# Attention with turned weights against scores made a second time in turned form, on one core

## The reference

```
h = attention(x): 16 heads of 32; q, k, v = x Wq', x Wk', x Wv'
    scores = q k' / sqrt(32);  scores = -inf where mask (512 x 512, one for all batches)
    o = softmax(scores) v;  o = o Wo'
    h = o / rms(o) * rms_scale * (1 + sc[b]) + shift[b]     (sc, shift from the conditioning)
x = x + h
x = x + quaternion rotation of x with a spectral gate       (a fixed 512 x 512 map, 4 x 4 blocks)
```

## Time and profile before

| | us |
|---|---|
| median of the runs | 988.85 |
| span of the profiled execution | 986.2 |
| median less span | 2.7 |
| TensorE matmul busy | 912.2 (92%) |
| TensorE weight load busy | 648.2 (66%) |
| VectorE busy | 707.5 (72%) |
| ScalarE busy | 638.8 (65%) |
| GpSimd busy | 523.6 (53%) |

### The profile page before, as it was taken

The page is one execution under the profiler, slowest core; times in us unless marked ns, Lnnn a source line. Parts: engine busy times, 40 slices in busy tenths (PEclk is TensorE's granted clock), DMA queues, the critical chain, the costliest instruction groups (busy, mean ns, idle before and its releaser), DMA issues.

```text
span 986.2 us, 20466 instructions
## 1 busy us (share of the span) xinstructions
PE 912.2 (92%) x6278; PEld 648.2 (66%) x6278; DVE 707.5 (72%) x1581; ACT 638.8 (65%) x1523; POOL 523.6 (53%) x441
## 2 busy tenths in 40 slices
PE   7999999999968989999999998999999999999980
PEld 5788888888845557666666665666666666666650
DVE  4522132223168888989999898899999899898878
ACT  5222222223158888888888887788888888888820
POOL 0999930000001122677666776566677666776665
PEclk9999999999979999999999999999999999999995
DMA  8855465544878547756666745666665576455111
GB/s 282 303 188 193 170 223 189 183 171 181 186 249 185 118 98 181 164 117 151 150 140 139 194 108 129 152 155 145 142 161 125 133 187 156 109 120 139 33 54 43
DMA packets 82325, 153.98 MB, mean 156 GB/s; under 512 B 8472, under 2 KB 9112, under 8 KB 82224
## 3 DMA queue, kind: packets, MB, share of 16 engines
q1 hardware_dynamic: 82224, 152.75, 57.6%
HBM read 102.35 MB, written 50.36 MB: 155 GB/s over the span
## 4 chain that ended last, share of the span: by engine, by line
PE 59%; issue 6%; DVE 5%; POOL 1%; DVEq 0%; ACT 0%; POOLq 0%
PE prob_ps L663 27%; PE out_ps L679 15%; PE score_ps L647 12%; DVE probs_T L770 2%; PE y_ps L700 2%; PE y_ps L701 1%; PE y_ps L702 1%; PE out_ps L689 1%; DVE probs L528 1%; POOL probs L1008 1%; DVE probs L754 0%; DVE probs L824 0%; DVE probs L836 0%; DVEq L520 0%; DVE probs L831 0%
## 5 line engine op out<-in xcount | busy, mean ns | idle before, releaser
L867 ACT ACTIVATE probs<-probs,least 128x512 f32<-128x512 f32 x512 | 364.3, 716 | 32.0 <-DVE inv_den L763 25.4
L663 PE MATMUL prob_ps<-ident,probs 128*128 128x128 f32 x2048 | 314.5, 281 | 26.2 <-DVE probs_T L770 25.4
L754 DVE CUSTOM_DVE_ANT_0 probs<-score_ps,mask_bias 128x512 f32<-128x512 f32 x512 | 333.1, 679 | 4.4 <-PE score_ps L647 4.4
L663 PEld LDWEIGHTS prob_ps<-ident,probs 128*128 128x128 f32 x2048 | 227.4, 141 | 159.2 <-issue 117.7
L647 PE MATMUL score_ps<-k_rows,q_rows 128*128 128x512 f32 x512 | 240.4, 477 | 12.5 <-PEq L78 9.3
L770 DVE COPY probs_T<-prob_ps 128x512 f32<-128x512 f32 x256 | 175.4, 685 | 65.0 <-PE prob_ps L663 63.1
L874 ACT ACTIVATE probs_T<-prob_ps 128x512 f32<-128x512 f32 x256 | 153.2, 598 | 76.7 <-PE prob_ps L663 72.6
L271 DVE SCALAR_TENSOR_TENSOR late<-proj,late 128x512 fp32r<-128x512 f32 x64 | 44.0, 690 | 181.3 <-ACT late L240 181.2
L679 PE MATMUL out_ps<-probs_T,v_sb 128*32 128x256 f32 x2048 | 163.0, 391 | 0.0
L528 POOL TENSOR_TENSOR late<-rot,late 128x2048 f32<-128x2048 f32 x26 | 119.1, 4580 | 66.8 <-DVE late L787 66.8
L940 POOL TENSOR_TENSOR o_T<-raw_T 128x256 f32<-128x256 f32 x64 | 47.9, 748 | 142.3 <-ACT raw_T L882 142.3
(11 more groups left out here) (112 smaller groups left out, 1349.1 us busy)
## 6 DMA issues: line engine op xcount, KB each, us to landing
q_rows<-q_scratch SPq DMA_DIRECT2D x128, 256.0 KB, 5.8
k_rows<-k_scratch SPq DMA_DIRECT2D x128, 256.0 KB, 6.7
q_scratch<-late SPq DMA_DIRECT2D x64, 256.0 KB, 2.3
k_scratch<-late SPq DMA_DIRECT2D x64, 256.0 KB, 2.3
v_scratch<-v_out SPq DMA_DIRECT2D x32, 256.0 KB, 2.0
v_sb<-v_scratch SPq DMA_DIRECT2D x8, 1024.0 KB, 10.9
raw<-in_xT SPq DMA_DIRECT2D x7, 1024.0 KB, 5.6
late<-in_x SPq DMA_DIRECT2D x28, 256.0 KB, 2.7
```

What stands on the lines that cost most here:

```text
L663: last = pe.transpose(prob_ps[:, r % 2, j * HALF + c * P:j * HALF + (c + 1) * P], probs[:, s % 2, r // 2 * 2 + c, key:key + P], ident[:, :])
L754: dve.tensor_tensor_reduce(probs[:, s % 2, r, :], score_ps[:, r % 4, :], mask_bias[:, c, :], 1.0, 3e38, ALU.add, ALU.min, least[:, s % 2, ...
L867: act.activation(probs[:, s % 2, r, :], probs[:, s % 2, r, :], ACT.Exp, bias=least[:, s % 2, r:r + 1], scale=-1.0, accum_out=den[:, s % 2, ...
```

## The change

The scores of a tile are now made twice. First with queries in the partitions, only for the minimum of each row: VectorE's instruction writes its other output back into the same PSUM bank (`row_least`). The minima are split in two parts, turned by TensorE, and transferred into two further rows of q, against rows of -1 in k. Then the scores are made a second time with the keys in the partitions: ScalarE has copied the turned mask into the bank before (`set_mask`), and the matmul of 98 rows adds to it (`start=False`). The exponential has no bias and no accumulator, and its output is already the turned weights, which `value` takes 512 queries at a time. `turn`, `move_out`, `invert` and `turn_scale` go. The sums of the weights come from TensorE, with a matrix of ones, on sums of two tiles that VectorE makes (`pair_up`, `total`); they are turned by VectorE in 32 x 32 blocks. There are no device loops in the attention stage. A unit has 16 places `t`. Row scores run 23 tiles ahead in two banks, the second scores have three banks, the weights a ring of 12.

```diff
-        for r in range(4):
+    def load(self, sp, u):
+        p = u % RB
+        for r in range(3):
...
+        maskT_words = sb("maskT_words", [P, TC, S // 4], mybir.dt.int32)
+            link(dve.tensor_scalar(maskT_bias[:, :, :], maskT_u8, MASKED, None, ALU.mult))
...
+RB = 3
+RING, BANKS = 12, 3
+AHEAD, TURN_AFTER = 23, 18
+VALUE_AT, PROJECT_AT, SQUARE_AT = 3, 8, 15
+RESCALE_AT, SUMS_AT, VALUES_AT, RESIDUAL_AT = 5, 6, 7, 12
+PAIR_AT, TOTAL_AT = (1, 9), (12, 4)
...
+        def row_place(n):
+            return n + max(0, (n - TURN_AFTER - 1 + TILES) // TILES)
+        def turn_place(u):
+            return min(TILES * u + TURN_AFTER + 1, TILES * U) + u
...
+            load_v(0)
+            load_unit(2)
+            load_least(0)
+            for u in range(U):
...
+                    load_unit(u + 2)
...
+                    load_least(u + 1)
...
+            def row_scores(n):
...
+                if row_place(n) >= 2:
+                    pe.wait_ge(row_taken, row_place(n) - 1)
+                pe.matmul(row_ps[:, row_place(n) % 2, :], rows.q[u % RB][0:3 * D, i, c * P:(c + 1) * P],
+                          rows.k[u % RB][0:3 * D, i, :], start=True, stop=True).then_inc(row_filled, 1)
+            def turn_least(u):
+                pe.wait_ge(parts_ready, u + 1)
+                pe.wait_ge(row_taken, turn_place(u) - 1)
+                for c in range(TC):
+                    last = pe.transpose(row_ps[:, turn_place(u) % 2, c * P:(c + 1) * P], least_parts[:, c, :], ident[:, :])
+                last.then_inc(row_filled, 1)
+            def score(u, t):
...
+                pe.wait_ge(mask_set, TILES * u + t + 1)
+                pe.matmul(score_ps[:, (TILES * u + t) % BANKS, :], rows.k[u % RB][0:3 * D + 2, i, j * P:(j + 1) * P],
+                          rows.q[u % RB][0:3 * D + 2, i, :], start=False, stop=True,
+                          skip_group_check=True).then_inc(scored, 1)
...
+            def total(u, half):
+                pe.wait_ge(paired_up, 2 * u + half + 1)
...
+                for i in range(HG):
+                    last = pe.matmul(sum_ps[i * D:(i + 1) * D, :], ones[:, :], pair_sum[:, i, :],
+                                     start=(half == 0), stop=(half == 1))
...
+            for u in range(U):
+                for t in range(TILES):
+                    n = TILES * u + t + AHEAD
+                    if n < TILES * U:
+                        row_scores(n)
+                    if n % TILES == TURN_AFTER % TILES and u + 1 < U:
+                        turn_least(u + 1)
+                    score(u, t)
+                    if t % HG == VALUE_AT and TILES * u + t >= HG + VALUE_AT:
+                        done = TILES * u + t - HG - VALUE_AT
+                        value(done // TILES, done % TILES // HG)
+                    if t == TOTAL_AT[1] and u > 0:
+                        total(u - 1, 1)
+                    if t == TOTAL_AT[0]:
+                        total(u, 0)
+                    if u >= NG and PROJECT_AT <= t < PROJECT_AT + 6:
+                        for part in (2 * (t - PROJECT_AT), 2 * (t - PROJECT_AT) + 1):
+                            project(u - NG, part)
...
+            def row_least(n):
...
+                bank = row_ps[:, row_place(n) % 2, :]
+                dve.tensor_tensor_reduce(bank, bank, mask_bias[:, c, :], 1.0, 3e38, ALU.add, ALU.min,
+                                         least[:, u % 2, c, i:i + 1]).then_inc(row_taken, 1)
+            def split_least(u):
...
+                dve.tensor_copy(least_parts[:, :, 0:2 * HG:2].bitcast(F32R), least[:, u % 2]).then_inc(hi_split, 1)
+                dve.wait_ge(hi_split, u + 1)
+                dve.tensor_tensor(least_parts[:, :, 1:2 * HG:2].bitcast(F32R), least[:, u % 2],
+                                  least_parts[:, :, 0:2 * HG:2], ALU.subtract).then_inc(parts_ready, 1)
...
+                dve.tensor_copy(least_rows[:, :], row_ps[0:2 * HG, turn_place(u) % 2, :]).then_inc(row_taken, 1)
+            def turn_sums(u):
+                dve.wait_ge(totalled, 2 * (u + 1))
+                dve.transpose(sums_T[:, :, :].rearrange("p n d -> p (n d)"), sum_ps[:, :]).then_inc(sums_turned, 1)
+                dve.wait_ge(sums_turned, u + 1)
+                dve.reciprocal(inv[:, :], sums_T[:, :, 0]).then_inc(inverted, 1)
+            def pair_up(n):
+                dve.wait_ge(exped, 2 * HG * (n + 1))
...
+                dve.tensor_tensor(pair_sum[:, :, :], weights[:, first:first + HG, :], weights[:, second:second + HG, :],
+                                  ALU.add).then_inc(paired_up, 1)
+            def scale_values(u):
+                dve.wait_ge(valued, TC * (u + 1))
...
+                dve.transpose(inv_T[:, :].rearrange("p (n d) -> p n d", d=D),
+                              inv[:, :].unsqueeze(2).to_broadcast([P, S // D, D])).then_inc(inv_turned, 1)
...
+                dve.tensor_tensor(o_T[:, u % 2], value_ps[:, :], inv_T[:, :], ALU.mult).then_inc(o_scaled, 1)
...
+            for u in range(U):
+                for t in range(TILES):
+                    n = TILES * u + t + AHEAD
+                    if n < TILES * U:
+                        row_least(n)
+                    if n % TILES == TILES - 1 and u + 1 < U:
+                        split_least(n // TILES)
+                    if n % TILES == TURN_AFTER % TILES and u + 1 < U:
+                        take_rows(u + 1)
+                    if t in PAIR_AT and TILES * u + t > TILES // 2:
+                        pair_up(2 * u + PAIR_AT.index(t) - 1)
+                    if t == RESCALE_AT and u > NG:
+                        rescale(u - NG - 1)
+                    if t == SUMS_AT and u > 0:
+                        turn_sums(u - 1)
+                    if t == VALUES_AT and u > 0:
+                        scale_values(u - 1)
+                    if t == RESIDUAL_AT and u > NG:
+                        residual(u - NG - 1)
...
+            def set_mask(n):
+                if n >= BANKS:
+                    act.wait_ge(exped, n - BANKS + 1)
+                act.activation(score_ps[:, n % BANKS, :], maskT_bias[:, n % TILES // HG, :], ACT.Copy).then_inc(mask_set, 1)
+            def exp(n):
+                act.wait_ge(scored, n + 1)
...
+                act.activation(weights[:, n % RING, :], score_ps[:, n % BANKS, :], ACT.Exp, scale=-1.0).then_inc(exped, 1)
...
+                    exp(n)
+                    if n >= 1 and n + BANKS - 1 < TILES * U:
+                        set_mask(n + BANKS - 1)
+                    if t == SQUARE_AT and u >= NG:
+                        square(u - NG)
...
+            for u in range(U):
+                if u > NG:
+                    rms(u - NG - 1)
+                if u > 0:
+                    split(u - 1)
+                if u > NG:
+                    rotate(u - NG - 1)
+                if u >= NG:
+                    shift(u - NG)
```

More of the change, by code:

```diff
@@ L704, in project @@
+                if part == 11:
                     last.then_inc(y_ready, 1)
[L706 to L724 removed]
@@ L741, in _ @@
+            value(U - 1, TC - 1)
+            total(U - 1, 1)
+            pe.wait_ge(exped, TILES * U)
             for c in range(TC):
[L742 to L743 removed]
+                for part in range(12):
+                    project(CHUNKS + c, part, tail_y[c])
         @block.vector
         def _(dve):
[L747 to L755 removed]
@@ L807, in _ @@
-            for r in range(TILES + MASK_AHEAD):
-                mask(0, r // TILES, r % TILES)
-            batch(0, 0, first=True)
-            batch(1, 1)
-            with dve.Fori(2, B - 3, 2) as b:
-                batch(b, 0)
-                batch(b + 1, 1)
-            batch(B - 2, 0)
-            batch(B - 1, 1, last=True)
-            rescale(B - 2, 0, TC - 1)
+            dve.memset(ones[:, :], 1.0).then_inc(consts_set, 1)
+            dve.memset(least_parts[:, :, :], 0.0).then_inc(consts_set, 1)
```

595 lines of the change are left out of this document (221 added, 374 removed).

## The result

| | before | after |
|---|---|---|
| median of the runs, us | 988.85 | 1302.17 (1301.26 to 1303.8) |
| ratio | | 1.317 (95% interval 1.315 to 1.320) |
| span of the profiled execution | 986.2 | 1300.4 |
| TensorE / VectorE / ScalarE busy | 912 / 708 / 639 | 1053 / 784 / 634 |
| mean granted clock | 0.98 | 0.83 |

The change made the kernel 32% slower. The direction was forecast; the size (1149 us, range 1055 to 1215) was not. The clock before is the mean of its page: in the loop it was 0.99.

A forecast was written before the change was run, and what follows sets the result against it. TensorE bound the old kernel at 20.60 us per unit; a TensorE-VectorE lockstep would replace that. 279.6 + 22 + 4 x 22.9 + 26 x 25.95 + 22 + 17 + 40 + 2.7 gave 1149 us, range 1055 to 1215.

The forecast's parts named there:

- The first four units: Attention units without projection or rescale: 21.6 us each in lockstep, 22.9 with the split meeting GpSimd.
- The 2.7 us around the span: Added to the stage sum: the earlier median of 988.85 less the profiled execution's span of 986.2.
- The walk: Following TensorE's and VectorE's fixed orders through a unit's 16 places, coupled by two row banks: 23.65 us per unit.
- t=5 to turn: Leg on VectorE from t=5 to t=10, 8.7 us, plus 0.75 until TensorE may turn the minima.
- the split's collision: VectorE's splits of the minima at t=8 meet GpSimd's split on the shared port: 1.25 us later (0 to 2.0).
- rival B: TensorE's clock also falls, in each stand before the turn of the minima, 1.7 us per unit; total 1228 us; chance 0.18.
- a stand of 3.2 us: TensorE's idle time at a loop jump in the old trace, with a slow clock behind it; the clock rival's evidence.
- The port: VectorE waits for GpSimd on the shared SBUF port: 1.25 us at the minima's splits, 1.05 at the pair sum.
- t=1 to t=5: Leg with VectorE's row minimum and pair sum, then TensorE's row 4, score and totals: 5.7 us.
- turn to t=1: Leg where TensorE alone is late, from the turn of the minima: 8.0 us, plus 0.5 to VectorE.
- Rival C: Engine orders slide past one another, a unit costs VectorE's own 18.9 us; total 939 us; chance 0.10.
- the 23.65 us: Forecast lockstep time of one unit with projection and rescale, before the shared port's delays.

The follow-up runs named there:

- value_later: Changed kernel with TensorE issuing a unit's first value group at t=10 instead of t=7; 1228.65 us, ratio 1.244.
- no_mask: Changed kernel with ScalarE's mask copies left out, so a score waits only for a free bank; 1296.02 us, ratio 1.311.
- later_no_rotation: Changed kernel with the first value group at t=10 and GpSimd's rotation in the loop replaced by a copy; 1167.6 us, ratio 1.182.
- totals_later: Changed kernel without pair sums (TensorE sums the weights in four totals per unit) and with the first value group at t=10; 1110.68 us, ratio 1.124.
- half_pair_sums: On top of value_later, each pair sum is issued as two halves, at t and t+1; 1152.03 us, ratio 1.164.

## Why the prediction was wrong

**The stages.** The stage began at 279.8 us (forecast 279.6), the first exponential came at 303.0 (301.6). The first four units took 27.4 us each (22.9), the next 26 took 30.74 (25.95). What follows the last exponential (1251.3 us) took 49 us (40). So 1.4 + 18 + 124.5 + 9 = 153 us of miss: the loop is 143 of it. The 2.7 us around the span, too, were not what lies around a span: every run whose own span is on record, of the kernel before too, is 1.7 to 1.9 longer than that span. That term was 0.9 us too large.

**The failed step** is "I followed both orders through 16 places t of a unit and kept, at each place, the later of 'engine free' and 'other side released'". The walk released TensorE by row banks only. `value(u, 0)`, which TensorE issues at t=7, writes the bank that VectorE's `scale_values`, also at t=7, must have read (`o_scaled`). Row score 8 is queued behind it, and VectorE waits for that. In t=5 to turn, 13.0 us stand against 9.45. value_later took the wait away and got 10.5, of which 1.0 is the split's collision, so 9.5 at full clock: the walk to 0.1.

**The clock** was given to rival B, at 1.7 us in the unit. That it would go was right; the place and the size were not. B had it fall in the stand before the turn of the minima, but in the unit shown that stand (1.62 us, until 732.15) left it at 1.00. It fell behind the pair sum of t=1, at a stand of 1.76 us, and stayed at 0.50 through the wait for `o_T`, over 13 us; in other units it came back in between and fell again behind that wait (0.50 from 620 to 626 and from 630 to 636 us). Fillers recovered 2.9 us per unit, 69 us in the run. I had asked for a stand of 3.2 us, the one that the old trace showed. The length of one stand alone does not decide: in the same place of value_later one of 1.75 us (until 687.63) left the clock at 1.00, and behind one of 1.17 us (until 515.52) it was 0.50 from 516 us. The Trainium skill (TensorE: Matmul & The Clock Gate, "A second HAM failure mode: psum-queue depth-cycling") describes, for bfloat16 matmuls of 512 columns, short idle times between groups of matmuls, in a loop that cycles through banks, which make the clock go up and down. This trace, of float32 matmuls, agrees: 0.50 from 716 to 728 us and 1.00 at 729, in a unit of 31. I had cited the section before it, and took long gaps to be the condition.

**The port.** Pair sum: forecast 1.05 (half of 2.1), measured 1.62 in every unit from the fifth on, since the pair sum starts 0.6 us after GpSimd's addition each time; an order that closes on itself does not miss at random, so a half was no choice. Split of the minima: forecast 1.25, measured 0, then 1.0 once value_later had removed the wait. In each collision shown the one that came second waited: the pair sum for the addition of 2.36 us that was under way, and GpSimd's next addition in turn for the pair sum (3.20 us, 1.28 before); the prediction has only VectorE wait. The contention was priced right for VectorE; where it strikes was set by the wait that I missed. Its full price is 92 us, since the stand that it lengthens costs the clock as well.

**The balance of the unit**, 30.74 against 25.95: t=1 to t=5 +2.1 (port 0.6 more, the rest clock); t=5 to turn +2.3 (wait and its clock +3.6, less the 1.25 of the split); turn to t=1 +0.4 (half of it ScalarE, which TensorE waits for 0.33 and 0.27 us in a unit: no_mask has 8.7 there).

**What held.** Row minima 0.61 us apart, also when they write PSUM; a group of eight 1.00 to its successor (1.17 forecast); mask copies and exponentials 0.49 apart in a queue; the two pair sums 2.29 when alone. The walk's own legs: 5.7, 9.45 and 8.5 us forecast, 5.9 (later_no_rotation), 9.5 (value_later less the collision) and 8.9 (all with a full clock) measured. Rival C, the faster one, is refuted: even totals_later is at 23.9 us per unit.

**Not settled.** No kernel has all three terms removed without a side effect, so the 23.65 us stand on legs from different kernels. The first four units' extra 4.5 us and the 9 us at the end were not taken apart. Nor was the condition under which the clock falls: in value_later a stand of 1.75 us left it at 1.00 and one of 1.17 us did not.

## What to carry to other kernels

When two engines run fixed orders, list every semaphore that either waits for, and walk with all of them: the release of an accumulator bank that is written once a unit is as much a link as the ring of banks. A long instruction on the engine that feeds another is worth cutting in two before anything else (77 us here, for the same work), since it is the wait of the other engine, and with it the clock. And price a contention by what it does to the order, not by its own microseconds: removing one wait here brought a collision back.

## What the runs showed of the hardware that I had not expected

- The granted clock of the changed kernel fell to 0.50 at a stand of TensorE of 1.76 us and stayed there from about 715 to 729 us, and it fell in unit after unit. In value_later a stand of 1.75 us (until 687.63) left it at 1.00, one of 1.17 us (until 515.52) did not. In half_pair_sums, whose stand before the turn is 1.34 us, the loop's clock was 0.98.
- Matmuls of zeros in TensorE's stands raised it to 0.98 and took 69 us off.
- GpSimd's last addition of the rotation, 1.28 us before, takes 3.06 on average beside VectorE's pair sum (3.20 at 712.47 us): both sides pay, each for the other's instruction that was under way.
